# Spreading k's rows with a 0/1 matmul in an attention and feed-forward kernel

## The chip, the cores and the metric

The kernel runs on one core of a Trainium2 chip. The metric is device time in microseconds. The notes on each instruction come from one profiled execution of the kernel before.

## The reference, cut to what matters

One transformer layer on `x` of 4096 tokens by 256, all in float32:

```
q, k, v = x@Wq.T+bq, x@Wk.T+bk, x@Wv.T+bv      # 16 heads of 16 columns each
q, k    = rope(q), rope(k)                     # (xr, xi) -> (xr*c - xi*s, xr*s + xi*c)
x = layernorm(x + (softmax(q @ k.T / 16) @ v) @ Wo.T)
x = layernorm(x + ffn(x))                      # 256 -> 1024 -> 1024 -> 1024 -> 256
```

## The kernel before

There are three stages, each a block of five engine programs with a barrier behind it: `project` (L78), `attend` (L327), `feed_forward`. Constants: CH = 512 tokens in a chunk, NCH = 8 chunks, P = 128, HD = 16, FT = 2 halves of the 256 features, PAIRS = 8 pairs of heads.

`project` makes four *items* in each chunk, m = 0 to 3: q and k of the first feature half, q and k of the second (t = m % 2 is 1 for k). An item is [128 features, 512 tokens].

- PE (L216): for each item two float32 matmuls into `ps[m]` (each is two MATMUL instructions in the trace), then v for the chunk (`ps_v`, L239, L242).
- ACT (L255): the item's bias, `ps` to `item` (L262), and the copies of v to `v_all` (L269). There is a ring of four `item` and `ps` buffers; the bias of item n waits until item n-4 is split (`low_done`).
- DVE (L295) and POOL (L212): the rotation. DVE swaps neighbours (L303) and multiplies by the cosines (L305), POOL multiplies the swapped copy by the sines, DVE adds (L309). The rotated item is then split into a rounded *high* part (L287) and the *rest* (L292). The split of item n-1 is written inside item n: its high part behind L305, its rest behind L309 of item n.
- SP (L142): loads x and the tables; stores both parts of every item, q's and k's, to DRAM (`store`, L153) and reads k's back (`place`, `place_k`, L67), six DMAs for each k item. A `parts` buffer is free again only when its store has landed, and there is one for q and one for k. At the end SP waits for all of it (L195, L197).

`place_k` lays the rows out as the scores need them. `k_all` has two halves of 64 partitions, one for each head of a pair: 48 rows of k (high, rest, high of its 16 features), then three rows of ones, then 13 that nothing reads. The last k item is placed at the start of `attend` (L422), and the ones are written there by two DMAs from a buffer that POOL fills (L464, L430).

`attend` works in 32 units of (chunk, group of four heads). PE makes all the scores once for the row maxima (`wide`, L507), which DVE reduces (L646); the negated maxima go through POOL into three rows of `q_sb` (L413); PE makes the scores again with those rows (L572), ACT takes the exponential (L624), PE sums with v (L532). At its start stand 64 groups of maxima of unit 0 and the first 8 of unit 1; only then comes `unit(0, 0)`. SP's order there: q (L75), the last of k (L67), more q, the ones (L430), a copy of the feed-forward weights (L432), then, for each unit, some words of those weights (L439) and the shift rows (L413). DVE's scan of the words (L666) stands between the maxima of units 0 and 1.

Of the kernel before, what the change touches and what calls it, by code (L numbers as in the profile page):

```python
# [16 lines left out]
F32 = mybir.dt.float32  # L17
# [39 lines left out]
PLACES = PAIR * len(K_PART)  # L57


def place_k(sp, k_parts, k_all, c, ft, done):  # L60
    cols = bass.ds(c * CH, CH)
    pairs = slice(ft * PAIRS // FT, (ft + 1) * PAIRS // FT)
    for e in range(PAIR):
        for r, part in enumerate(K_PART):
            src = k_parts[part].rearrange("(j e d) s -> e d j s", e=PAIR, d=HD)[e]
            at = e * HALF + r * HD
            sp.dma_start(k_all[at:at + HD, pairs, cols].bitcast(F32), src[:, pairs, cols]).then_inc(done, 16)  # L67
# [10 lines left out]
def project(nc, io, parts_dram, v_all, k_all):  # L78

    with ExitStack() as ctx:
# [9 lines left out]
        RING = 4  # L96
# [9 lines left out]
        parts = [sb(f"parts{b}", [P, 2, CH], F32R) for b in range(2)]  # L106
# [16 lines left out]
        parts_free = [sem(f"parts_free{b}") for b in range(2)]  # L123
        k_in = sem("k_in")
        v_ready = sem("v_ready")
        v_free = sem("v_free")
        waited = sem("project_waited")
        sp_waited = sem("sp_waited")
        ones_set = sem("ones_set")

        ITEMS = 2 * FT
        TOTAL = NCH * ITEMS

        def started(n):

            return not isinstance(n, int) or 0 <= n < TOTAL
# [4 lines left out]
        def _(sp):  # L141
            def load(p, c):  # L142
                cols = bass.ds(c * CH, CH)
# [4 lines left out]
            def store(c, m):  # L148

                ft, t = m // 2, m % 2  # L150
                sp.wait_ge(low_done, RING + c * ITEMS + m + 1)
                dst = parts_dram[t].rearrange("a f s -> f a s")[ft * P:(ft + 1) * P]
                sp.dma_start(dst[:, :, bass.ds(c * CH, CH)], parts[t][:].bitcast(F32)).then_inc(parts_free[t], 16)  # L153

            def place(c, ft):

                sp.wait_ge(parts_free[1], 16 + (c * FT + ft + 1) * 16)
                sp.sem_inc(sp_waited, 1)
                place_k(sp, parts_dram[1], k_all, c, ft, k_in)

            def chunk(c, first=False):
                store(c, 0)
                if not first:
                    place(c - 1, 1)
                store(c, 1)
                store(c, 2)
                place(c, 0)
                store(c, 3)

            sp.dma_start(w_sb[:, 0], io["wqT"].rearrange("(t p) o -> p t o", p=P)).then_inc(w_in, 16)  # L170
            load(0, 0)
# [7 lines left out]
            load(1, 1)  # L179
            chunk(0, first=True)  # L180
            sp.wait_ge(v_ready, 2)
            load(0, 2)
            chunk(1)
            sp.wait_ge(v_ready, 4)
            load(1, 3)
            with sp.Fori(1, NCH // 2 - 1) as cc:
                for p in range(2):
                    chunk(cc * 2 + p)


                    sp.wait_ge(v_ready, (cc * 2 + p + 1) * 2)
                    load(p, cc * 2 + p + 2)
            chunk(NCH - 2)
            chunk(NCH - 1)
            for b in range(2):  # L195
                sp.wait_ge(parts_free[b], 16 + 16 * TOTAL // 2)
            sp.wait_ge(k_in, 16 * PLACES * (NCH * FT - 1))  # L197

        @block.gpsimd
        def _(pool):  # L200
            pool.memset(v_all[:, :, :, :, HD:HD + 1], 1.0).then_inc(ones_set, 1)
            pool.wait_ge(ones_set, 1)
            pool.memset(one_row[:], 1.0).then_inc(ones_set, 1)
            pool.wait_ge(ones_set, 2)
            with pool.Fori(0, NCH // 2) as cc:
                for p in range(2):
                    pool.wait_ge(table_in[p], cc * 32 + 32)
                    for m in range(ITEMS):
                        n = (cc * 2 + p) * ITEMS + m

                        pool.wait_ge(swapped, n + 1)
                        pool.tensor_tensor(pair[m % 2][:], pair[m % 2][:], table[p][:, 1], ALU.mult).then_inc(sine_done, 1)  # L212

        @block.tensor
        def _(pe):
            def chunk(c, p):  # L216
                for m in range(ITEMS):
                    ft, t = m // 2, m % 2
                    n = c * ITEMS + m
                    if isinstance(c, int) and c == 0 and m < 2:  # L220

                        pe.wait_ge(w_in, 16 * (t + 1))
                    if started(n - RING):

                        pe.wait_ge(biased, n - RING + 1)
                    for i in range(FT):
                        last = pe.matmul(ps[m][:], w_sb[:, t, i, ft * P:(ft + 1) * P], xt[p][:, i],  # L227
                                         start=(i == 0), stop=(i == FT - 1))
                    last.then_inc(projected, 1)
                if isinstance(c, int) and c == 0:  # L230
                    pe.wait_ge(v_weights_in, 32)
                    pe.wait_ge(ones_set, 2)
                for a in range(2):

                    pe.wait_ge(v_free, c * 2 + a + 1)
                    for b in range(2):
                        tt = 2 * a + b
                        for i in range(FT):
                            pe.matmul(psv[a][:, b], xt[p][:, i, tt * P:(tt + 1) * P], wv_sb[:, i],  # L239
# [5 lines left out]
            for p in range(2):  # L245
                pe.wait_ge(x_in[p], 16)
                chunk(p, p)
            with pe.Fori(1, NCH // 2) as cc:
                for p in range(2):
                    pe.wait_ge(x_in[p], cc * 16 + 16)  # L250
                    chunk(cc * 2 + p, p)

        @block.scalar
        def _(act):
            def chunk(c):  # L255
                for m in range(ITEMS):
                    ft, t = m // 2, m % 2
                    n = c * ITEMS + m
                    act.wait_ge(projected, n + 1)

                    act.wait_ge(low_done, n + 1)
                    act.activation(item[m][:], ps[m][:], ACT.Identity, bias=b_sb[:, t, ft:ft + 1]).then_inc(biased, 1)  # L262
                    if m >= ITEMS - 2:

                        a = m - (ITEMS - 2)
                        act.wait_ge(v_ready, c * 2 + a + 1)
                        for b in range(2):
                            dst = v_all[:, :, bass.ds(c * TT + 2 * a + b, 1), :, 0:HD]
                            last = act.activation(dst.rearrange("p g a j d -> p (g a) j d"),  # L269
                                                  psv[a][:, b].rearrange("p (g j d) -> p g j d", g=NG, j=HG), ACT.Copy)  # L270
                        last.then_inc(v_free, 1)

            act.wait_ge(b_in, 32)
            chunk(0)
            chunk(1)
            with act.Fori(2, NCH) as c:
                chunk(c)
            act.wait_ge(v_free, 2 + 2 * NCH)

        @block.vector  # L280
        def _(dve):
            def high(n, b):

                if started(n):
                    dve.wait_ge(rotated, n + 1)
                    dve.wait_ge(parts_free[b % 2], (n - b % 2) * 8 + 16)
                    dve.tensor_copy(parts[b % 2][:, 0], item[b][:]).then_inc(high_done, 1)  # L287

            def low(n, b):
                if started(n):  # L290
                    dve.wait_ge(high_done, n + 1)
                    dve.tensor_tensor(parts[b % 2][:, 1], item[b][:], parts[b % 2][:, 0].bitcast(F32), ALU.subtract)\  # L292
                        .then_inc(low_done, 1)

            def chunk(c, p):  # L295
                for m in range(ITEMS):
                    n = c * ITEMS + m
                    if started(n - 2):
# [3 lines left out]
                    dve.sem_inc(waited, 1)  # L302
# [3 lines left out]
                    high(n - 1, (m - 1) % RING)  # L306
# [3 lines left out]
                    low(n - 1, (m - 1) % RING)  # L310

            dve.sem_inc(low_done, RING)
            dve.sem_inc(v_free, 2)
            for b in range(2):
                dve.sem_inc(parts_free[b], 16)
            for p in range(2):
                dve.wait_ge(table_in[p], 32)
                chunk(p, p)
            with dve.Fori(1, NCH // 2) as cc:
                for p in range(2):  # L320
                    dve.wait_ge(table_in[p], cc * 32 + 32)
                    chunk(cc * 2 + p, p)
# [924 lines left out]
```

## Time and profile before

| what | us |
|---|---|
| median of 3 runs | 3895.44 (3888.07 to 3899.75) |
| the profiled execution | 3898.05 |
| its span, first to last instruction | 3896.5 |
| PE, DVE, ACT busy in the span | 3556.2, 2932.8, 2469.0 |
| granted PE clock, mean | 0.939 of full |

Busy shares are means over stages with different limits. The stages in the trace: `project` to 173 us, `attend` from 173.5 us, `feed_forward` at the end.

### The profile page before, as it was taken

The numbers are of one execution on the slowest core, as the hardware profiler recorded it, in microseconds if no ns is written. First come the engines' busy times: TensorE is split into PE (matmuls) and PEld (weight loads), VectorE is DVE, ScalarE is ACT, GpSimd is POOL, SyncE is SP. The second block draws the span as 40 slices with busy tenths as digits, with TensorE's granted clock in tenths as the row PEclk, the third lists the DMA queues.
The fourth block names the chain that finished last, engine by engine and source line by source line (L and its number), as shares of the span: only waits on it lengthen the run. The fifth ranks groups of instructions, "written<-read, shape, count | busy, mean of one in ns | idle before, by whom it ended". The sixth has DMA issues, their size and how long they took to land. (4 is left out here: it accounts for less than half of the span.)

```text
span 3896.5 us, 63480 instructions
## 1 busy us (share of the span) xinstructions
PE 3556.2 (91%) x20130; PEld 1524.5 (39%) x20130; DVE 2932.8 (75%) x3148; ACT 2469.0 (63%) x4472; POOL 197.3 (5%) x352
## 2 busy tenths in 40 slices
PE   7679999999999999999999999999988869999999
PEld 3222333332333323332332333222222148888887
DVE  6688888888888888888888888888886035445554
ACT  2118888877778878887877887778787522222222
POOL 3200000000000000000000000000000011111100
PEclk9759999999999999999999999999999579999999
DMA  8940000000000000000000000000000051000100
GB/s 212 201 133 12 12 12 12 12 12 12 23 12 12 12 12 12 12 12 13 22 12 12 12 12 12 12 12 12 12 14 4 0 181 34 34 33 33 49 17 12
DMA packets 64516, 125.61 MB, mean 32 GB/s; under 512 B 12551, under 2 KB 24904, under 8 KB 63032
## 3 DMA queue, kind: packets, MB, share of 16 engines
q1 hardware_dynamic: 59528, 114.02, 10.4%
q0 software_dynamic: 4704, 7.81, 0.7%
q8 instruction: 177, 2.90, 0.3%
q14 instruction: 107, 0.88, 0.1%
HBM read 90.59 MB, written 41.16 MB: 34 GB/s over the span
## 5 line engine op out<-in xcount | busy, mean ns | idle before, releaser
L646 DVE TENSOR_REDUCE group_max<-wide 128x2 f32<-128x1024 f32 x2048 | 2405.8, 1220 | 365.2 <-PE wide L507 364.3
L624 ACT ACTIVATE probs<-scores 128x512 f32<-128x512 f32 x4096 | 2227.1, 596 | 583.8 <-PE scores L572 491.6
L572 PE MATMUL scores<-q_sb,k_all 51*128 51x512 f32 x4096 | 1064.7, 516 | 197.5 <-ACT probs L624 60.3
L532 PE MATMUL sums<-probs,v_all 128*17 128x512 f32 x8192 | 1135.0, 627 | 0.0
L572 PEld LDWEIGHTS scores<-q_sb,k_all 51*128 51x128 f32 x4096 | 395.8, 190 | 1460.2 <-ACT probs L624 1362.7
L507 PE MATMUL wide<-k_all,q_sb 48*128 48x512 f32 x4096 | 809.2, 461 | 75.5 <-DVE group_max L646 49.2
L507 PEld LDWEIGHTS wide<-k_all,q_sb 48*128 48x128 f32 x4096 | 404.3, 194 | 381.9 <-DVE group_max L646 347.7
L1029 ACT ACTIVATE whole_hid<-acc,scale 128x512 f32<-128x512 f32 x128 | 84.9, 690 | 346.5 <-PE acc L910 344.9
L910 PE MATMUL acc<-hid_b,h2T 128*128 128x512 f32 x1024 | 241.6, 396 | 0.0
L910 PE MATMUL acc<-hid_a,h1T 128*128 128x512 f32 x1024 | 240.2, 394 | 0.0
L532 PEld LDWEIGHTS sums<-probs,v_all 128*17 128x17 f32 x8192 | 137.1, 96 | 262.5 <-ACT probs L624 197.3
L910 PEld LDWEIGHTS acc<-hid_b,h2T 128*128 128x128 f32 x1024 | 192.2, 188 | 46.5
L910 PEld LDWEIGHTS acc<-hid_a,h1T 128*128 128x128 f32 x1024 | 191.7, 187 | 47.2
L1119 DVE CAST hid_a<-whole_hid 128x512 fp32r<-128x512 f32 x128 | 54.5, 426 | 185.5 <-ACT whole_hid L1029 183.4
L474 POOL CAST shift_parts<-shift 16x128 bf16<-16x128 f32 x32 | 9.1, 285 | 2741.6 <-ACT shift L617 2662.9
L1020 ACT ACTIVATE gate<-acc,scale 128x512 f32<-128x512 f32 x64 | 44.3, 691 | 125.2 <-PE acc L910 120.8
L1180 DVE TENSOR_SCALAR flag<-flip 1x1 int32<-1x1 f32 x1 | 0.1, 145 | 147.2 <-PE flip L997 147.2
L227 PE MATMUL ps_qk<-xt,w_qk 128*128 128x512 f32 x128 | 73.4, 738 | 26.7 <-DMA xt<-in_xT 26.7
L1121 DVE TENSOR_TENSOR hid_a<-whole_hid,hid_a 128x512 fp32r<-128x512 f32 x128 | 88.7, 693 | 4.4
L1128 DVE SCALAR_TENSOR_TENSOR whole_hid<-acc,scale,gate 128x512 f32<-128x512 f32 x64 | 48.0, 750 | 45.3 <-PE acc L910 45.2
L883 PE MATMUL tok<-wo,heads_sb 128*128 128x256 f32 x256 | 58.7, 389 | 18.0 <-DVE heads_sb L1094 18.0
L910 PE MATMUL acc<-x1t,w1T 128*128 128x512 f32 x256 | 71.8, 402 | 2.1 <-DVE x1t L1113 2.1
(77 smaller groups left out, 1158.4 us busy)
## 6 DMA issues: line engine op xcount, KB each, us to landing
k_all<-k_parts SPq DMA_DIRECT2D x96, 128.0 KB, 5.0
q_sb<-q_parts SPq DMA_DIRECT2D x192, 64.0 KB, 2.3
w_words<-ff_weights SPq DMA_DIRECT2D x32, 352.0 KB, 3.2
q_parts<-parts SPq DMA_DIRECT2D x16, 512.0 KB, 5.7
k_parts<-parts SPq DMA_DIRECT2D x16, 512.0 KB, 6.2
heads<-mixed SPq DMA_DIRECT2D x32, 256.0 KB, 2.5
heads_sb<-heads SPq DMA_DIRECT2D x8, 1024.0 KB, 4.9
shares<-shares_dram POOLq DMA_DIRECT2D x112, 64.0 KB, 2.2
```

Of the source, the lines that this page charges most:

```text
L227: last = pe.matmul(ps[m][:], w_sb[:, t, i, ft * P:(ft + 1) * P], xt[p][:, i], start=(i == 0), stop=(i == FT - 1))
L507: last = pe.matmul(wide[n % 2][:, e], q_sb[g][rows, j, t * P:(t + 1) * P], k_all[rows, g * GP + j, b * CH:(b + 1) * CH], start=True, stop= ...
L532: last = pe.matmul(sums[32 * j:32 * j + HD + 1, :], v_all[:, g, kt, j], probs[(kt * HG + j) % RING][:], start=(kt == 0), stop=(kt == KT - 1))
L572: pe.matmul(scores[(s + e) % BANKS][:], k_all[rows, g * GP + j, kt * P:(kt + 1) * P], q_sb[g][rows, j], start=True, stop=True).then_inc(sc ...
L624: act.activation(probs[n % RING][:], scores[s % BANKS][:], ACT.Exp, scale=INV_SCALE)\
L646: dve.reduce_max(group_max[:, n], wide[n % 2][:], AX_X).then_inc(wide_free, 1)
L883: last = pe.matmul(tok[t // 2][:, t % 2], heads[:, g, t * P:(t + 1) * P], wo[:, g], start=(g == 0), stop=(g == NG - 1))
L910: mm = pe.matmul(dst, w.bitcast(view), src[h].bitcast(view), start=(first and h == 0), stop=(last and h == 1))
L1029: act.activation(whole[o % 4][:], acc[n % 4][:], ACT.Gelu, scale=scale[:, 2 + layer, o:o + 1])\
L1119: dve.tensor_copy(dst[0][:, k % HT], whole[k % 4][:]).then_inc(rounded, 1)
L1121: dve.tensor_tensor(dst[1][:, k % HT], whole[k % 4][:], dst[0][:, k % HT].bitcast(F32), ALU.subtract)\
L1128: dve.scalar_tensor_tensor(out=whole[o % 4][:], in0=acc[(2 * o + 1) % 4][:], scalar=scale[:, 1, o:o + 1], in1=gate[o % 2][:], op0=ALU.mult ...
```

## The change

k's parts stay on the chip. `choose` is a 0/1 matrix, [128, 2, 128]: for each pair of heads j, its 32 rows by 128 columns send the high and rest rows of two heads to their places in a [128, 512] PSUM tile. ACT copies that tile to `k_all` with a bias of one in the rows of ones. The matrix is made at the start by POOL and DVE. q still goes through DRAM. All loops over chunks in `project` are written out. The items' order against the new `spread_k` is the same on PE and ACT. Cut to its core (`load`, the item's own operations and what only lost its register arithmetic are left out):

```diff
-def place_k(sp, k_parts, k_all, c, ft, done):
...
-        RING = 4
+        RING, SPREADS = 4, 2
+        spread = [psum(f"ps_spread{b}", [P, CH]) for b in range(SPREADS)]
...
+            for c in range(NCH):                         # sync
+                for ft in range(FT):
+                    sp.wait_ge(low_done, c * ITEMS + 2 * ft + 1)
+                    dst = q_dram.rearrange("a f s -> f a s")[ft * P:(ft + 1) * P]
+                    sp.dma_start(dst[:, :, c * CH:(c + 1) * CH], parts[0][:].bitcast(F32)).then_inc(q_stored, 16)
+                if c + 2 < NCH:
+                    sp.wait_ge(v_ready, 2 * c + 2)
+                    sp.wait_ge(rotated, (c + 1) * ITEMS)
+                    load(c + 2)
+            sp.wait_ge(q_stored, 16 * NCH * FT)
...
+            def spread_k(c, ft):                         # tensor; JP = 4
+                if c == 0 and ft == 0:
+                    pe.wait_ge(choose_set, 5)
+                pe.wait_ge(low_done, c * ITEMS + 2 * ft + 2)
+                for j in range(JP):
+                    i = (c * FT + ft) * JP + j
+                    rows = slice(j * PAIR * HD, (j + 1) * PAIR * HD)
+                    if i >= SPREADS:
+                        pe.wait_ge(spread_free, i - SPREADS + 1)
+                    for a in range(2):
+                        last = pe.matmul(spread[i % SPREADS][:], choose[rows, a], parts[1][rows, a],
+                                         start=(a == 0), stop=(a == 1))
+                    last.then_inc(spread_ready, 1)
+            for c in range(NCH):
+                pe.wait_ge(x_in[c % 2], (c // 2 + 1) * 16)
+                item_of(c, 0)
+                item_of(c, 1)
+                if c > 0:
+                    spread_k(c - 1, 1)
+                item_of(c, 2)
+                item_of(c, 3)
+                values(c)
+                spread_k(c, 0)
+            spread_k(NCH - 1, 1)
...
+            def spread_k(c, ft):                         # scalar
+                for j in range(JP):
+                    i = (c * FT + ft) * JP + j
+                    act.wait_ge(spread_ready, i + 1)
+                    act.activation(k_all[:, ft * JP + j, c * CH:(c + 1) * CH], spread[i % SPREADS][:], ACT.Identity,
+                                   bias=ones_rows[:]).then_inc(spread_free, 1)
...
+            def high(n):                                 # vector
+                t, b = n % 2, n % RING
+                dve.wait_ge(rotated, n + 1)
+                if t == 0 and n >= 2:
+                    dve.wait_ge(q_stored, 16 * (n // 2))
+                if t == 1 and n >= 2:
+                    dve.wait_ge(spread_ready, JP * (n // 2))
+                dve.tensor_copy(parts[t][:, 0], item[b][:]).then_inc(high_done, 1)
...
-            place_k(sp, k_parts, k_all, NCH - 1, FT - 1, k_in)      # attend
-            sp.wait_ge(ones_set, 1)
-            (two DMAs of ones into k_all, and the waits on k_in and k_ones)
```

ACT's loop over chunks has the same order as PE's: bias 0, bias 1, `spread_k(c - 1, 1)`, bias 2, bias 3, the copies of v, `spread_k(c, 0)`.

## Rows read from the trace of the kernel before

**Rows 1.** Busy time by stretch, within project (us, engines, clock, DMA).

```profile
39.01:44.76 5.75, 5.75 (x7) 2.52 (x8) 5.12 (x11) 0.69 (x1) 1.93 (x2) 0.50 1.08 250
58.33:61.80 3.47, 3.47 (x4) 1.45 (x5) 1.66 (x4) 0.00 (x0) 1.77 (x1) 0.51 1.07 300
77.64:97.86 20.22, 15.97 (x41) 7.83 (x41) 13.22 (x25) 3.97 (x8) 7.08 (x4) 0.84 1.01 235
```

**Rows 2.** Waits in 20 to 175 us: who, for whom, us, times, longest.

```profile
DVE parts L287 <- DMA k_parts<-parts: 35.0, 14, 3.5
PE ps_qk L227 <- DMA xt<-in_xT: 20.9, 6, 4.2
```

**Rows 3.** Timeline of PE, projections by chunk: start, length, [idle before it].

```profile
21.77 7.13 PE L227 MATMUL ps_qk<-xt,w_qk 128*128 128x512 f32 x16
39.01 9.97 PE L227 MATMUL ps_qk<-xt,w_qk 128*128 128x512 f32 x16 [3.56 <-DMA xt<-in_xT]
58.33 8.82 PE L227 MATMUL ps_qk<-xt,w_qk 128*128 128x512 f32 x16 [2.81 <-DMA xt<-in_xT]
137.04 8.74 PE L227 MATMUL ps_qk<-xt,w_qk 128*128 128x512 f32 x16 [3.25 <-DMA xt<-in_xT]
```

**Rows 4.** Timeline, all engines, of the first chunks.

```profile
23.07 0.72 DVE L303 STREAM_SHUFFLE pair<-item 128x512 f32<-128x512 f32 x1
...
23.79 0.69 ACT L262 ACTIVATE item<-ps_qk,b_qk 128x512 f32<-128x512 f32 x1 [1.25 <-PE ps_qk L227]
...
25.51 0.69 ACT L262 ACTIVATE item<-ps_qk,b_qk 128x512 f32<-128x512 f32 x1 [1.03 <-PE ps_qk L227]
...
26.44 0.68 DVE L292 TENSOR_TENSOR parts<-item,parts 128x512 fp32r<-128x512 f32 x1
...
27.05 0.71 DVE L303 STREAM_SHUFFLE pair<-item 128x512 f32<-128x512 f32 x1
...
28.74 1.03 PE L239 MATMUL ps_v<-w_v,xt 128*128 128x256 f32 x4
...
34.75 0.69 PE L242 MATMUL ps_v<-b_v,one_row 1*128 1x256 f32 x2
...
35.48 0.66 ACT L269 ACTIVATE v_all<-ps_v 128x256 f32<-128x256 f32 x2 [2.13 <-PE ps_v L242]
```

**Rows 5.** Timeline of PE in attend: fp32r matmuls at half clock, then at full.

```profile
182.79 0.80 PE L507 MATMUL wide<-k_all,q_sb 48*128 48x512 f32 x2 [0.34 <-DVE group_max L646]
...
278.70 1.05 PE L532 MATMUL sums<-probs,v_all 128*17 128x512 f32 x8
279.69 0.50 PE L572 MATMUL scores<-q_sb,k_all 51*128 51x512 f32 x2
280.02 0.70 PE L507 MATMUL wide<-k_all,q_sb 48*128 48x512 f32 x4
```

**Rows 6.** Waits of SP's own queue, 0 to 280 us.

```profile
SPq L197 <- DMA k_parts<-parts: 5.9, 1, 5.9
```

**Rows 7.** Timeline, all engines, first load and first matmul of attend.

```profile
173.52 2.65 SPq L75 DMA_DIRECT2D q_sb<-q_parts  x6
...
178.43 1.22 PE L507 MATMUL wide<-k_all,q_sb 48*128 48x512 f32 x4 [26.09 <-DMA q_sb<-q_parts]
```

**Rows 8.** Timeline, all engines, from the ones to attend's first unit.

```profile
187.92 1.76 SPq L430 DMA_DIRECT2D k_all<-mixed  x2
...
254.02 0.37 SPq L439 DMA_DIRECT2D w_words<-ff_weights  x1
255.87 4.22 SPq L413 DMA_DIRECT2D q_sb<-shift_rows  x6
257.04 0.89 DVE L666 SCALAR_TENSOR_TENSOR bits<-w_words,bits 128x704 int32<-128x704 int32 x1 [4.40 <-DMA w_words<-ff_weights]
257.85 11.40 DVE L646 TENSOR_REDUCE group_max<-wide 128x2 f32<-128x1024 f32 x10
...
264.94 0.34 PEld L572 LDWEIGHTS scores<-q_sb,k_all 51*128 51x128 f32 x2
```

More of the change, by code:

```diff
@@ L56 @@
 SLOT = SHIFT_ROW + 3
-PLACES = PAIR * len(K_PART)
-def place_k(sp, k_parts, k_all, c, ft, done):
[L61 to L67, printed above, removed]
+PLACES = PAIR * len(Q_PART)
 def place_q(sp, q_parts, q_sb, c, g, done):
@@ L75, in place_q, with project @@
             sp.dma_start(q_sb[at:at + HD].bitcast(F32), src[:, g * GP:(g + 1) * GP, bass.ds(c * CH, CH)]).then_inc(done, 16)
-def project(nc, io, parts_dram, v_all, k_all):
+def project(nc, io, q_dram, v_all, k_all):
     with ExitStack() as ctx:
@@ L105, in project @@
         pair = [sb(f"pair{b}", [P, CH]) for b in range(2)]
-        parts = [sb(f"parts{b}", [P, 2, CH], F32R) for b in range(2)]
+        parts = [sb(f"parts{t}", [P, 2, CH], F32R) for t in range(2)]
+        eye = sb("eye", [P, P])
+        same = sb("same", [P, PAIR * HD])
+        choose = sb("choose", [P, 2, P], F32R)
+        ones_rows = sb("ones_rows", [P, 1])
         ps = [psum(f"ps_qk{b}", [P, CH]) for b in range(RING)]
         psv = [psum(f"ps_v{a}", [P, 2, D]) for a in range(2)]
+        spread = [psum(f"ps_spread{b}", [P, CH]) for b in range(SPREADS)]
         w_in = sem("w_qk_in")
@@ L122, in project @@
         low_done = sem("low_done")
-        parts_free = [sem(f"parts_free{b}") for b in range(2)]
-        k_in = sem("k_in")
+        q_stored = sem("q_stored")
+        spread_ready = sem("spread_ready")
+        spread_free = sem("spread_free")
         v_ready = sem("v_ready")
         v_free = sem("v_free")
-        waited = sem("project_waited")
-        sp_waited = sem("sp_waited")
         ones_set = sem("ones_set")
+        eye_set = sem("eye_set")
+        choose_set = sem("choose_set")
         ITEMS = 2 * FT
         TOTAL = NCH * ITEMS
-        def started(n):
-            return not isinstance(n, int) or 0 <= n < TOTAL
+        JP = PAIRS // FT
         block = ctx.enter_context(nc.Block())
@@ L141, in _, with load @@
         def _(sp):
-            def load(p, c):
-                cols = bass.ds(c * CH, CH)
+            def load(c):
+                cols, p = slice(c * CH, (c + 1) * CH), c % 2
                 sp.dma_start(xt[p][:], io["xT"].rearrange("(t p) s -> p t s", p=P)[:, :, cols]).then_inc(x_in[p], 16)
@@ L146, in load @@
                     sp.dma_start(table[p][:, n], io[name][:, cols]).then_inc(table_in[p], 16)
[L148 to L168, printed above, removed]
             sp.dma_start(w_sb[:, 0], io["wqT"].rearrange("(t p) o -> p t o", p=P)).then_inc(w_in, 16)
-            load(0, 0)
+            load(0)
             for n, name in enumerate(["bq", "bk"]):
@@ L178, in _ @@
             sp.dma_start(bv_sb[:], io["bv"].rearrange("(o d) -> o d", o=1)).then_inc(v_weights_in, 16)
[L179 to L197, printed above, removed]
+            load(1)
+            for c in range(NCH):
[8 more added lines that the diff above has]
+            sp.wait_ge(q_stored, 16 * NCH * FT)
         @block.gpsimd
@@ L203, in _ @@
             pool.memset(one_row[:], 1.0).then_inc(ones_set, 1)
[L204 to L212, printed above, removed]
+            pool.memset(eye[:], 0.0).then_inc(eye_set, 1)
@@ new lines, in _ @@
+            pool.memset(choose[:].bitcast(F32), 0.0).then_inc(choose_set, 1)
+            pool.wait_ge(eye_set, 1)
+            pool.affine_select(out=eye[:], in_=eye[:], compare_op=ALU.not_equal, fill=1.0, base=0,
+                               pattern=[[-1, P]], channel_multiplier=1).then_inc(eye_set, 1)
+            for c in range(NCH):
+                p = c % 2
+                pool.wait_ge(table_in[p], (c // 2 + 1) * 32)
+                for m in range(ITEMS):
+                    pool.wait_ge(swapped, c * ITEMS + m + 1)
+                    pool.tensor_tensor(pair[m % 2][:], pair[m % 2][:], table[p][:, 1], ALU.mult).then_inc(sine_done, 1)
@@ L214, in _, with item_of @@
         @block.tensor
         def _(pe):
[L216 to L230, printed above, removed]
+            def item_of(c, m):
+                ft, t, n = m // 2, m % 2, c * ITEMS + m
+                if c == 0 and m < 2:
+                    pe.wait_ge(w_in, 16 * (t + 1))
+                if n >= RING:
+                    pe.wait_ge(biased, n - RING + 1)
+                for i in range(FT):
+                    last = pe.matmul(ps[m][:], w_sb[:, t, i, ft * P:(ft + 1) * P], xt[c % 2][:, i],
+                                     start=(i == 0), stop=(i == FT - 1))
+                last.then_inc(projected, 1)
@@ L231, in chunk, with values @@
+            def values(c):
+                if c == 0:
                     pe.wait_ge(v_weights_in, 32)
@@ L238, in chunk @@
                         for i in range(FT):
-                            pe.matmul(psv[a][:, b], xt[p][:, i, tt * P:(tt + 1) * P], wv_sb[:, i],
+                            pe.matmul(psv[a][:, b], xt[c % 2][:, i, tt * P:(tt + 1) * P], wv_sb[:, i],
                                       start=(i == 0), stop=False)
@@ L243, in chunk @@
                     last.then_inc(v_ready, 1)
[L245 to L251, printed above, removed]
+            def spread_k(c, ft):
[11 more added lines that the diff above has]
+                    last.then_inc(spread_ready, 1)
@@ L253, in _ @@
+            for c in range(NCH):
+                pe.wait_ge(x_in[c % 2], (c // 2 + 1) * 16)
+                item_of(c, 0)
+                item_of(c, 1)
+                if c > 0:
+                    spread_k(c - 1, 1)
[4 more added lines that the diff above has]
+            spread_k(NCH - 1, 1)
         @block.scalar
         def _(act):
[L255 to L271, printed above, removed]
@@ L273, in _, with bias @@
-            act.wait_ge(b_in, 32)
[L274 to L278, printed above, removed]
+            def bias(c, m):
+                ft, t, n = m // 2, m % 2, c * ITEMS + m
+                act.wait_ge(projected, n + 1)
+                if n >= RING:
+                    act.wait_ge(low_done, n - RING + 1)
+                act.activation(item[m][:], ps[m][:], ACT.Identity, bias=b_sb[:, t, ft:ft + 1]).then_inc(biased, 1)
@@ new lines, in values @@
+            def values(c):
+                for a in range(2):
+                    act.wait_ge(v_ready, c * 2 + a + 1)
+                    for b in range(2):
+                        dst = v_all[:, :, c * TT + 2 * a + b, :, 0:HD]
+                        last = act.activation(dst, psv[a][:, b].rearrange("p (g j d) -> p g j d", g=NG, j=HG), ACT.Copy)
+                    last.then_inc(v_free, 1)
+            def spread_k(c, ft):
[4 more added lines that the diff above has]
+                                   bias=ones_rows[:]).then_inc(spread_free, 1)
@@ L280, in _ @@
+            act.wait_ge(b_in, 32)
+            act.wait_ge(choose_set, 6)
+            for c in range(NCH):
+                bias(c, 0)
+                bias(c, 1)
+                if c > 0:
+                    spread_k(c - 1, 1)
+                bias(c, 2)
+                bias(c, 3)
+                values(c)
+                spread_k(c, 0)
+            spread_k(NCH - 1, 1)
+            act.wait_ge(v_free, 2 * NCH)
+            act.wait_ge(spread_free, NCH * FT * JP)
         @block.vector
         def _(dve):
[L282 to L295, printed above, removed]
+            def high(n):
[6 more added lines that the diff above has]
+                dve.tensor_copy(parts[t][:, 0], item[b][:]).then_inc(high_done, 1)
@@ new lines, in low @@
+            def low(n):
+                t, b = n % 2, n % RING
+                dve.wait_ge(high_done, n + 1)
+                dve.tensor_tensor(parts[t][:, 1], item[b][:], parts[t][:, 0].bitcast(F32), ALU.subtract)\
+                    .then_inc(low_done, 1)
+            dve.wait_ge(eye_set, 2)
+            dve.wait_ge(choose_set, 1)
+            dve.reduce_max(same[:], eye[:].rearrange("p (j x) -> p x j", x=PAIR * HD), AX_X).then_inc(choose_set, 1)
+            dve.wait_ge(choose_set, 2)
+            for r, part in enumerate(K_PART):
+                dst = choose[:, part].rearrange("p (e r d) -> p e r d", e=PAIR, d=HD)[:, :, r]
+                dve.tensor_copy(dst, same[:].rearrange("p (e d) -> p e d", e=PAIR)).then_inc(choose_set, 1)
@@ L296, in chunk @@
+            by_half = eye[:].rearrange("p (e x) -> p e x", e=PAIR)[:, :, SHIFT_ROW:SLOT]
+            dve.reduce_max(ones_rows[:], by_half, mybir.AxisListType.XY).then_inc(choose_set, 1)
+            for c in range(NCH):
+                p = c % 2
+                dve.wait_ge(table_in[p], (c // 2 + 1) * 32)
                 for m in range(ITEMS):
                     n = c * ITEMS + m
-                    if started(n - 2):
+                    if n >= 2:
                         dve.wait_ge(rotated, n - 1)
@@ L309, in chunk, with attend @@
                     dve.tensor_tensor(item[m][:], item[m][:], pair[m % 2][:], ALU.add).then_inc(rotated, 1)
[L310 to L322, printed above, removed]
-            high(TOTAL - 1, (TOTAL - 1) % RING)
-            low(TOTAL - 1, (TOTAL - 1) % RING)
-def attend(nc, io, q_parts, k_parts, heads_dram, w_dram, low_bits, v_all, k_all):
+                    if n >= 1:
+                        low(n - 1)
+            high(TOTAL - 1)
+            low(TOTAL - 1)
+def attend(nc, io, q_parts, heads_dram, w_dram, low_bits, v_all, k_all):
     with ExitStack() as ctx:
@@ L421, in _ @@
             load_q(0, 0)
-            place_k(sp, k_parts, k_all, NCH - 1, FT - 1, k_in)
             for g in range(1, NG):
                 load_q(0, g)
-            sp.wait_ge(ones_set, 1)
-            for e in range(PAIR):
-                at = e * HALF + SHIFT_ROW
-                rows = k_all[at:at + 3].rearrange("a j (c s) -> a (j c) s", s=CH)
-                src = mixed[0][0:3].unsqueeze(1).to_broadcast([3, PAIRS * NCH, CH])
-                sp.dma_start(rows.bitcast(F32), src).then_inc(k_ones, 16)
             for name, (at, rows, cols) in W_AT.items():
@@ L517, in max_start @@
             def max_start(c, g):
-                if not isinstance(c, int) or g >= NG // FT:
-                    pe.wait_ge(k_in, 16 * PLACES)
                 pe.wait_ge(q_in[g], c * (16 * PLACES) + 16 * PLACES)
@@ L1197, in build @@
 def build(nc, io, out):
-    parts_dram = [nc.dram_tensor(f"{t}_parts", [2, D, S], F32, kind="Internal").ap() for t in "qk"]
+    q_dram = nc.dram_tensor("q_parts", [2, D, S], F32, kind="Internal").ap()
     heads_dram = nc.dram_tensor("heads", [NCH, P, NG, CH], F32, kind="Internal").ap()
@@ L1206, in build @@
             with nc.sbuf_tensor("k_all", [P, PAIRS, S], F32R) as k_all:
-                project(nc, io, parts_dram, v_all, k_all)
-                attend(nc, io, *parts_dram, heads_dram, w_dram, low_bits, v_all, k_all)
+                project(nc, io, q_dram, v_all, k_all)
+                attend(nc, io, q_dram, heads_dram, w_dram, low_bits, v_all, k_all)
         feed_forward(nc, io, heads_dram, shares_dram, w_dram, low_bits, out)
```

11 lines of the change are left out of this document (3 added, 8 removed).

## The prediction

> **What bounds the kernel now.** I read the table of stretches first, then the waits, then the timeline of a chunk, then the two ends of the stage.
>
> `attend` and `feed_forward` hold 3723 of the 3896.5 us. The change touches them at `attend`'s start alone: the loops keep their instructions but for a wait that has long been met. So the question is how long `project` lasts and how `attend` starts.
>
> In `project` the chunks begin 19.6 us apart: (137.04 - 39.01)/5 [rows 3]. DMA sets that. Its engines are busy for all of a chunk (share 1.01) at 235 GB/s [rows 1], DVE waits 35.0 us for k's stores to land, and PE 20.9 us for x [rows 2]. PE alone would need less: at full clock one item takes 25.51 - 23.79 = 1.72 us, and the v part runs from 28.74 to 34.75 + 0.69 = 35.44, 6.7 us [rows 4], so a chunk 4 x 1.72 + 6.7 = 13.6 us. DVE and POOL need 27.05 - 23.07 = 3.98 us an item [rows 4], 15.9 us a chunk. After each wait for x PE's granted clock is at the lower level (0.50, 1.2 GHz) for 3.5 to 5.8 us of dense work [rows 1]; idle stretches of 2.81 and of 3.56 us both went before it [rows 3].
>
> **What goes.** In each chunk two stores of k (512 KB each) and twelve reads back (128 KB each), 2.5 MB of 4.5 MB. What stays, 2 MB (1 MB of x and tables, two q stores), is 9 us at 235 GB/s, hidden in any chunk of 20 us. DVE's wait for k's landings goes. If nothing else bound the chunk, DVE would, at 15.9 us. What is late next is, I think, not an engine but a ring of orders.
>
> **What comes, and the ring.** The rest of item (c-1, 3) is made inside DVE's item (c, 0), behind its add. `spread_k(c-1, 1)` waits for it on PE, which works in order, so the items (c, 2) and (c, 3), v, `spread_k(c, 0)` and item (c+1, 0) are all queued behind that wait. DVE's item (c+1, 0), in which the next such rest is made, waits for the last of these. One turn of the ring is one chunk. I time it from the start of DVE's item (c, 0), S = 0, at full clock.
>
> - The rest is ready 26.44 + 0.68 - 23.07 = 4.05 us after the item's start [rows 4]; with some 0.1 to pass the semaphore, PE starts at 4.15.
> - A spread is two fp32r matmuls of 512 columns, one after the other in one bank. Two pairs take 0.70, one pair 0.50 [rows 5], so a stream of 512 columns costs some 0.215, and a spread 0.43; ACT starts 0.3 later (an item's end on PE against its bias: 21.77 + 1.72 against 23.79 [rows 3, 4]). The nearest row for the copy is the bias, PSUM to SBUF with a per-row operand, 0.69 [rows 4]; I let two in a row start 0.61 apart. With two buffers the third spread waits for the first copy. Copies start at 4.88, 5.49, 6.38 and 6.99; PE's four spreads end at 6.69, and not at 4.15 + 4 x 0.43 = 5.87.
> - Item 2 ends at 8.41, its bias runs 8.71 to 9.40, so DVE's item 2 starts at 9.54 (it could have at 7.96). Item 3 ends at 10.13, v at 16.83. `spread_k(c, 0)` needs the rest of item 1, ready at 13.6: no wait. Its first copy stands behind two copies of v (0.66 [rows 4]) and starts at 17.74; two buffers again, and PE ends its fourth spread at 19.54.
> - Item (c+1, 0) ends at 21.26, its bias runs 21.56 to 22.25, DVE starts at 22.39.
>
> That is 22.4 us for a chunk at full clock, against 19.6 now. If the spreads waited for no copy, 2 x 0.95 would go: 20.5, still over 19.6. Dearer spreads are bounded by a half-clock one, 0.85.
>
> Clock: item (c+1, 1) ends on PE at 22.98 and the next rest is ready at 26.54. PE is idle 3.6 us in every chunk, between the idle stretches that now go before the lower level [rows 3]. I take the same here: lower level for a mean of 4.7 us of work behind the gap (between the 3.5 and the 5.8 of [rows 1]). At half clock a pair takes 0.80 [rows 5]; a spread is 0.85, is ready 0.35 later, and the four end 3.67 after their start instead of 2.54: 1.13 lost. The 1.0 us left of the lower level falls on item 2: 0.5 lost. Together 1.65 (bounds: 0 where the clock stays, 2.9 where the lower level lasts 6.8 us).
>
> Between full-array matmuls and others PE loses a little: eight sums and the start of the next scores lie 0.99 apart where the sums stream for 4 x 0.215 = 0.86 [rows 5], 0.13 lost. A spread phase has two such borders, one of the four hidden behind the wait: 3 x 0.1 = 0.3 (bounds 0 and 0.4).
>
> The Trainium skill has a rule for this that speaks against the change: TensorEngine Tiling, "Key Properties", says that going from one tiling mode to another drains TensorE. The 0.13 us agrees with a small price; by that row all four borders would cost 0.5 us a chunk.
>
> So a chunk takes 22.4 + 1.65 + 0.3 = 24.35 us.
>
> **Start and end of the stage.** Chunk 0 goes as now up to DVE's item 2 at 23.07 - 3.98 = 19.1 [rows 4]: `choose` needs some ten small operations of POOL and DVE, which have nothing else to do before the first bias. The rest of item 1 comes at 23.1; spreads to 25.8, item (1, 0) to 27.5, DVE's item (1, 0) at 28.6 (now 27.05 [rows 4]). Item (7, 0) starts at 28.6 + 6 x 24.35 = 174.7. The last chunk ends with eight copies: PE's v at S + 18.5, copies from 19.4, the first four with starts 0.6 to 0.9 apart, the other four by 25.2. The last q store is issued at S + 19.2 and lands by 24 (SP now waits 5.9 us for k's last [rows 6]). Then some 0.9 for the barrier, an estimate: a few waits of the 0.1 us kind in a row, bounds 0.3 and 2. SP's first q load: 174.7 + 25.2 + 0.9 = 200.8, against 173.52 [rows 7]: 27.3 later.
>
> **`attend`'s start.** Six DMAs of k (2.7 us of SP's queue, as the six of q) and two of ones (1.76) go [rows 7, 8]. q's load to the first matmul, 4.9 us [rows 7], and the 64 groups of maxima stay, as DVE bounds them (1.14 us each by the ten at 257.85 [rows 8]). The copy of the weights is issued 4.5 us sooner after the first q load, and DVE's scan now waits 4.40 us for its words, whose load waited for that copy to 254.02 [rows 8]. So DVE resumes up to 4.2 us sooner. PE's first scores stand behind the 8 groups of unit 1 that DVE paces to 264.94; the shift rows, issued from 255.87 with 4.22 us of issue [rows 8], land near 262. I take 264.94 - 262.2 = 2.7 us gained (bounds 0 and 4.2). k's waits in the loops and the instructions of the written-out loops I take as nothing: PE's queue hides the former, and chunks 0 and 1, written out already, show no stall.
>
> **Sum.** +27.3 - 2.7 = +24.6. The profiled execution's 3898.05 becomes 3922.7; the median shown lies 2.6 lower, so 3920.
>
> **The rivals.**
>
> 1. *The clock stays at its upper level.* For it: the gap is shared between two stretches of work, and spreads begin at once. Against: 2.81 us were enough [rows 3]. Chunk 22.7, last chunk 23.5: item (7, 0) at 164.8, q load at 189.2, +15.7 - 2.7 = +13; 3908.
> 2. *The lower level covers more than I take*, since a spread uses 32 of 128 rows and waits for ACT between. Then `spread_k(c, 0)` and item (c+1, 0) run at half clock too: 1.13 + 1.72 = 2.85 more, less what overlaps: 26.5 to 27.2. Item (7, 0) at 28.6 + 6 x 26.9 = 190, +42.6 - 2.7 = +40; 3936. The fp32r matmuls at 182.79 stay at half clock though PE is idle 0.34 of each 1.13 us [rows 5], which speaks for it; the items between, dense for 10 us, against.
> 3. *The ring does not close*: the new time is that of the freed engines. The place is PE's wait ahead of item (c, 2); if the rest of (c-1, 3) came before PE gets there, a chunk would be PE's sum, 13.6 + 16 x 0.215 = 17.0, and the kernel faster. Item (7, 0) at 131, last chunk 23: q load at 155, -19 - 2.7 = -21; 3874. It decides below 19.6 us a chunk. The DMA share speaks for it [rows 1]; the order of DVE's program, in which that rest stands behind the add of an item that PE has yet to feed, against it.
> 4. *The change is lost in the noise*: copies cheaper than 0.69 and half-free spreads, a chunk near 20.5. Item (7, 0) at 151.6, q load at 176, +2 - 3 = 0; 3895.
>
> **How the numbers follow.** A difference under 0.3%, 11.7 us, can't be told from no change. The forecast 0.52, rival 1 0.17 (of which some 0.07 within 0.3%), rival 2 0.13, rival 3 0.08, rival 4 0.10. So slower 0.74, same 0.18, faster 0.08. The range takes in rivals 1 and 2 and the three runs' own spread of 12 us: 3903 to 3938.
>
> **What would show it.** In the new trace: DVE's items 0 of two chunks 24 us apart; its items 2 and 0 each waiting on ACT's bias, some 1.6 to 3.2 and 5 us; PE idle 3.6 us ahead of `spread_k(c-1, 1)` with DVE's L292 as releaser; half clock once a chunk; DMA share near 0.5; the first q load near 200; the scan's wait under 1 us. PE idle ahead of item 2 under 1 us, or chunks under 20 us apart, would prove the ring wrong; a stage of 24 us a chunk and a total within 12 us of now would prove the part on `attend` wrong.

## The result, and the profile after

The changed kernel takes 3963.73 us (3953.64 to 3969.86, 4 runs) against 3893.85 (4 runs) for the kernel before: 1.0178 [1.0155, 1.0202], slower by 70 us. I had forecast 3920, 25 us slower, in a range up to 3938. The sign was right, the size was not, and the time lies outside the range.

The page of the kernel after (span, busy, granted clock):

```profile
span 3964.0 us, 63316 instructions
PE 3623.9 (91%) x20258; PEld 1551.2 (39%) x20258; DVE 2953.4 (75%) x3153; ACT 2506.5 (63%) x4536; POOL 196.5 (5%) x354
PEclk8858999999999999999999999999998579999999
DMA  2240000000000000000000000000000051111100
```

The same row of the kernel before:

```profile
DMA  8940000000000000000000000000000051000100
```

DMA's share in the first two slices is 2 tenths, where it was 8 and 9: the transfers did go off the path. PE's mean clock is a little lower than before: 0.80 from 20 us to the end of `project`, against 0.83.

One chunk of `project` in the kernel after, from DVE's item (4, 0) to item (5, 0), then its pieces by clock. The columns are those of [rows 1]: the stretch, its length, the busy us of PE, PEld (weight loads), DVE, ACT and POOL with the number of instructions, PE's clock, DMA's share and GB/s:

```profile
113.04:140.34 27.30, 22.39 (x57) 10.53 (x57) 15.98 (x25) 9.12 (x16) 7.02 (x4) 0.81 0.23 77
112.00:118.80 6.80, 2.75 (x10) 1.01 (x9) 5.70 (x10) 2.26 (x4) 2.67 (x2) 1.00 0.00 1
118.80:125.60 6.80, 6.80 (x10) 2.94 (x11) 2.88 (x5) 2.43 (x4) 0.81 (x1) 0.50 0.20 77
125.60:135.90 10.30, 9.44 (x36) 5.25 (x35) 7.39 (x11) 3.76 (x9) 3.54 (x2) 1.00 0.20 55
135.90:139.30 3.40, 3.40 (x5) 1.33 (x6) 0.00 (x0) 0.67 (x2) 0.00 (x0) 0.51 0.86 296
```

A chunk takes 27.3 us, not 19.6 and not the 24.35 forecast. PE works at half clock in two stretches, 6.8 and 3.4 us; before there was one, of 3.4 or 6.8 us. DMA's share of a chunk is 0.23.

PE's timeline of that chunk, with its idle time before each group:

```profile
117.15 0.73 PE L220 MATMUL ps_spread<-parts,choose 32*128 32x512 f32 x4 [3.28 <-DVE parts L294]
118.65 1.80 PE L220 MATMUL ps_spread<-parts,choose 32*128 32x512 f32 x4 [0.77 <-ACT k_all L260]
120.38 6.28 PE L187 MATMUL ps_qk<-xt,w_qk 128*128 128x512 f32 x8
126.50 1.03 PE L202 MATMUL ps_v<-w_v,xt 128*128 128x256 f32 x4
...
134.53 1.31 PE L220 MATMUL ps_spread<-parts,choose 32*128 32x512 f32 x4 [0.86 <-ACT k_all L260]
135.77 5.40 PE L187 MATMUL ps_qk<-xt,w_qk 128*128 128x512 f32 x8
```

The ring is there: PE stands 3.28 us until DVE's rest (L294), 4.11 us after the start of DVE's item. The two items behind the spreads take 126.50 - 120.38 = 6.1 us, where they take 3.44 at full clock.

The waits of the kernel after in 20 to 240 us, against [rows 2]:

```profile
DVE pair L315 <- ACT item L245: 74.4, 14, 7.3
PE ps_spread L220 <- DVE parts L294: 26.3, 9, 3.3
PE ps_spread L220 <- ACT k_all L260: 13.0, 16, 0.9
```

DVE's waits for stores are gone; it waits 74.4 us for biases (items written by ACT) instead, in 14 places, some two a chunk.

The start of `attend` after, against [rows 7, 8] (timeline, SP and DVE):

```profile
224.07 13.03 SPq L65 DMA_DIRECT2D q_sb<-q_parts  x24
...
274.18 0.37 SPq L431 DMA_DIRECT2D w_words<-ff_weights  x1
...
303.20 0.87 DVE L652 SCALAR_TENSOR_TENSOR bits<-w_words,bits 128x704 int32<-128x704 int32 x1
306.51 4.21 SPq L412 DMA_DIRECT2D q_sb<-shift_rows  x6
...
311.89 0.80 PE L559 MATMUL scores<-q_sb,k_all 51*128 51x512 f32 x2 [0.18 <-DMA q_sb<-shift_rows]
```

The two spans differ by 3964.0 - 3896.5 = 67.5 us, and this is where they are. The first q load comes 224.07 - 173.52 = 50.5 later. From it to unit 0's shift rows both kernels take 82.4. From there to unit 1's it is 89.8 against 95.3: 5.5 gained. The next 30 units take 2658.5 against 2641.9: 16.6 lost. The end of `attend` takes 2.5 and the feed-forward (from its first load of x, at 3199.99 and 3135.79) 3.3 more. The 16.6 were in no step of mine:

```profile
PE wide L498 <- issue: 13.0, 6, 2.4
```

That is a row of the kernel after's waits in 330 to 2950 us: six times PE stands up to 2.4 us with nothing that it waits for. The kernel before has two such stalls there (`PE scores L572 <- issue: 7.2, 2, 3.7`). One of the six in the timeline of PE:

```profile
755.50 0.39 PE L498 MATMUL wide<-k_all,q_sb 48*128 48x512 f32 x1
758.28 1.22 PE L498 MATMUL wide<-k_all,q_sb 48*128 48x512 f32 x3 [2.39 <-issue]
758.98 0.94 PE L559 MATMUL scores<-q_sb,k_all 51*128 51x512 f32 x2
759.85 1.91 PE L519 MATMUL sums<-probs,v_all 128*17 128x512 f32 x8
```

It lies in the second group of matmuls of the loop's first unit, one loop turn (four units) from the next. Behind it eight sums take 1.91 us, not the 1.05 of [rows 5]: the clock has fallen.

### The profile page after: what moved, and what is told of

Its sections match the earlier page's. It is cut to its first block and busy times, and to the rows that moved or that the text cites. A ratio compares the mean times of both kernels' runs of the same rounds, so it can differ in the third digit from the quotient of the medians.

```text
span 3964.0 us, 63316 instructions
## 1 busy us (share of the span) xinstructions
PE 3623.9 (91%) x20258; PEld 1551.2 (39%) x20258; DVE 2953.4 (75%) x3153; ACT 2506.5 (63%) x4536; POOL 196.5 (5%) x354
## 5 line engine op out<-in xcount | busy, mean ns | idle before, releaser
L498 PE MATMUL wide<-k_all,q_sb 48*128 48x512 f32 x4096 | 817.9, 463 | 63.8 <-DVE group_max L632 44.3
L187 PE MATMUL ps_qk<-xt,w_qk 128*128 128x512 f32 x128 | 90.1, 868 | 6.0 <-DMA xt<-in_xT 6.0
L220 PE MATMUL ps_spread<-parts,choose 32*128 32x512 f32 x128 | 40.9, 534 | 39.2 <-DVE parts L294 26.3
```

What stands on the lines that cost most here:

```text
L498: last = pe.matmul(wide[n % 2][:, e], q_sb[g][rows, j, t * P:(t + 1) * P], k_all[rows, g * GP + j, b * CH:(b + 1) * CH], start=True, stop= ...
```

## The experiments

All were timed beside the kernel before on the same chip.

| kernel | us, median | ratio to before [95%] | a chunk | first q load | units 2 to 31 |
|---|---|---|---|---|---|
| after_again | 3966.68 | 1.0169 [1.0153, 1.0186] | 27.3 | 222.8 | 2660.4 |
| fill_gap | 3947.17 | 1.0128 [1.0112, 1.0145] | 27.3 | 219.2 | 2638.7 |
| fill_spread | 3933.82 | 1.0098 [1.0079, 1.0118] | 25.6 | 213.5 | 2632.4 |
| fill_all | 3913.70 | 1.0034 [1.0023, 1.0046] | 22.5 | 192.4 | 2644.2 |
| order | 3936.53 | 1.0099 [1.0082, 1.0116] | 21, 21, 26 | 195.0 | 2653.8 |
| early | 3929.23 | 1.0080 [1.0063, 1.0097] | 21 to 24 | 189.6 | 2651.7 |
| pad32 | 3943.13 | 1.0114 [1.0098, 1.0131] | 27.3 | 224.8 | 2636.9 |
| pad96 | 3959.87 | 1.0156 [1.0139, 1.0173] | 27.3 | 233.9 | 2647.4 |
| before_pad32 | 3902.18 | 1.0013 [1.0003, 1.0023] | 18.9 to 20.6 | 174.3 | 2642.7 |
| inter | 3879.20 | 0.9948 [0.9931, 0.9964] | 17.2 to 18.7 | 160.0 | 2636.4 |

"A chunk" is the distance of DVE's items 0 in the profile, in the later chunks; "units 2 to 31" goes from the first shift DMA of unit 1 to that of unit 31.

### after_again

> The changed kernel once more, for a second profile. All theories: some 70 us over the kernel before. Theory A (the projection costs 50 us, and the rest, +13 us in attend and +3 in the feed-forward, is the chance of where the clock's drops fall): the chunks of project lie 27.3 us apart again, the 30 later units of attend sum to anything from 2635 to 2665 us. Theory B (attend itself is slower by the change): they sum to 2658 again, within 5 us.

The chunks repeat at 27.3 us, with half clock twice a chunk, but not with the same drops: here each of the two lasts 6.8 us, 13.7 in all against 10.2, and the first begins at 115.9, just ahead of the spreads.

```profile
111.89:139.17 27.28, 23.19 (x57) 11.14 (x57) 15.97 (x24) 9.12 (x16) 7.01 (x4) 0.75 0.23 77
```

The units sum to 2660.4, inside what both theories allow, so the sum alone decides nothing. The six stalls are back, though (12.6 us): they belong to this program, not to one execution.

### fill_gap, fill_spread, fill_all

```diff
+            def fill(n, cols, times):                 # w_k stands here for k's weights, read as [128, 512]
+                pe.wait_ge(biased, n + 1)
+                for _ in range(times):
+                    pe.matmul(ps[n % RING][:, 0:cols], w_sb[:, 0, 0, 0:P], w_k[:, 0:cols], start=True, stop=True)
...
             def spread_k(c, ft):
+                if ft == 1 and c < NCH - 1:               # fill_gap, fill_all
+                    fill(c * ITEMS + 2, CH, 3)
                 pe.wait_ge(low_done, c * ITEMS + 2 * ft + 2)
...
                     last.then_inc(spread_ready, 1)
+                    if j == 1 and c < NCH - 1:            # fill_spread, fill_all
+                        fill(c * ITEMS + 2 * ft, CH // 2, 2)
```

> The changed kernel with three more float32 matmuls of 512 columns (2.6 us at full clock) on PE ahead of its wait for the rest of the last k item, into a ps bank that has been read; their results are overwritten. PE is idle 3.3 us there now, so they cost nothing in themselves. Theory A (the ring costs 22.7 us a chunk at full clock, and the lower clock behind the idle stretch and behind the spreads the other 4.6): the 6.8 us of half clock behind the gap go or shrink to 3.4, a chunk takes 24 to 25.5, the kernel 15 to 25 us less than the changed one. Theory C (spreads, their latency and their semaphores are dearer than I took, the clock is not it): a chunk stays at 27.3.

> As fill_gap, and in each spread phase two more float32 matmuls of 256 columns (0.43 us at full clock) between the second and the third spread, where PE waits 0.8 us for ACT. Theory A: no half clock in project after the first chunk, a chunk 22.5 to 23.5, the kernel 30 to 38 us less than the changed one. Theory C: 27.3 or more.

> The changed kernel with the two small filler matmuls between the second and the third spread alone, none in the 3.3 us gap. Theory G (it is the idle gap that takes the clock down, the spread phases only keep it down): the drop behind the gap stays, 24 to 26 us a chunk, the other one (behind the spreads that follow v) goes. Theory H (it is the spread phases, since in fill_gap, whose gap is filled, both drops stayed in the later chunks): close to fill_all's 22.5. Either way no stall of PE in attend is expected, since the program is longer: total 3915 to 3935.

A chunk by stretch in fill_gap (PE's wait for DVE's rest is down to 0.71 us):

```profile
135.49:162.79 27.30, 24.98 (x63) 11.68 (x62) 16.00 (x25) 9.13 (x16) 7.02 (x4) 0.81 0.23 78
```

And in fill_all:

```profile
98.64:121.15 22.51, 21.79 (x71) 11.20 (x71) 16.00 (x25) 9.02 (x16) 7.02 (x4) 1.00 0.28 92
```

fill_all decides: with PE kept busy in both places the granted clock is 1.00, and the chunk is the ring at full clock, 22.52 us. PE has more work, and the first q load comes 30 us sooner (222.8 to 192.4). The other 4.8 us of the changed kernel's chunk are the clock. The same 32-row spreads are in fill_all, so their few rows alone don't take the clock down. The total fell by 53 us against after_again, more than the 30 to 38 I expected: of the rest 16 us lie in units 2 to 31, where this longer program has one stall of 3.0 us and not six.

Filling the gap alone leaves the chunk at 27.3 (theory C's number, though not for its reason), and the clock still falls in the middle of the spreads. Filling the spreads alone gives 25.6 with one drop of 6.8 us a chunk, as theory G had it. So neither G nor H holds for both: spreads with waits of 0.8 us between them are enough for a drop (fill_gap), and so is the gap (fill_spread). fill_gap's total fell within my 15 to 25 us, but for another reason: 3.6 us by the first q load (two early chunks were short), and one stall in `attend` instead of six.

### order, early

order moves `spread_k(c - 1, 1)` behind item 3, on PE and on ACT:

```diff
                 item_of(c, 0)
                 item_of(c, 1)
-                if c > 0:
-                    spread_k(c - 1, 1)
                 item_of(c, 2)
                 item_of(c, 3)
+                if c > 0:
+                    spread_k(c - 1, 1)
```

early splits each chunk's last item at once, on DVE:

```diff
-                    if n >= 1:
+                    if n >= 1 and m > 0:
                         high(n - 1)
...
-                    if n >= 1:
+                    if n >= 1 and m > 0:
                         low(n - 1)
+                high(n)
+                low(n)
```

> The changed kernel with the spread of the previous chunk's last k item moved behind the four items on PE and behind the four biases on ACT. Theory A (the ring through DVE's rest, with PE in order, is what sets the chunk): the ring opens, PE's 3.3 us of idle go, a chunk is PE's own sum, 18.6 us at full clock and up to 20.5 with one drop; project ends 50 to 68 us sooner than in the changed kernel, the total is 3895 to 3915. Theory C: PE's work is the same, so a chunk gains at most the 3.3 us of idle, 24 us.

> The changed kernel with the split of each chunk's last k item right behind its add on DVE, not inside the next chunk's first item. Theory A (the ring): PE no longer waits for it, the ring is open as in order, a chunk is PE's sum of 18.6 us and what the lower clock adds, 21 to 24; total 3925 to 3940, the six stalls in attend included. Theory C (the order of PE's work): no gain, 27.3.

Either opens the ring, by two different edits: 28 and 33 us less by the first q load than after_again. PE's wait for DVE's rest between 40 and 190 us, in the changed kernel and then in order (in early it is the same row):

```profile
PE ps_spread L220 <- DVE parts L294: 16.4, 5, 3.3
PE ps_spread L220 <- DVE parts L294: 1.3, 1, 1.3
```

But they stop at 21 us a chunk and more, and order's total missed my 3895 to 3915; early's came inside its 3925 to 3940. In order one chunk in three takes 26.0, at a mean clock of 0.67:

```profile
99.21:125.20 25.99, 24.44 (x56) 11.97 (x55) 15.90 (x24) 9.10 (x16) 7.02 (x4) 0.67 0.28 97
```

PE is busy 24.44 of 25.99 us there and still at the lower level for the most part. Both keep the six stalls in `attend` (13.7 us each): their PE programs have as many instructions as the changed one.

### pad32, pad96, before_pad32

```diff
+            for _ in range(32):                          # 96 in pad96
+                pe.sem_inc(pad, 1)
             for c in range(NCH):
                 pe.wait_ge(x_in[c % 2], (c // 2 + 1) * 16)
```

> The changed kernel with 32 semaphore increments more in PE's program, at its start, where PE waits for x anyway. Theory F (some 17 us of the loss are in attend, because PE's program is now laid out so that six times, at the loop's turn, PE stands 1.6 to 2.4 us without an instruction, and the clock falls behind it; where the loop lies against the pieces in which instructions are fetched decides): a shift of the layout changes the number or length of these stalls, by as much as all: the 30 later units sum to 2640 where they are gone, the kernel 3945 to 3950; project stays at 27.3 us a chunk. Theory B (it is k_all written by ACT, or the chance of the clock): the stalls stay, 3963 to 3967.

> As pad32 with 96 increments, about as many instructions as fill_gap had more. Theory F: fill_gap had no such stall, so here too they go: 3945 to 3950. Theory B: 3963 to 3967.

> The kernel before with 32 semaphore increments more at the start of PE's program, where PE waits for x. Theory F (layout of PE's program against the pieces in which it is fetched): the stalls at the loop's turn in attend change, the total by anything from -5 to +22 us with project the same. If the kernel before happens to lie as well as it can, it is unchanged within 0.3% or slower. Theory B: unchanged.

32 instructions that do nothing take 0.55% off the kernel (1.0114 against 1.0169), 21 us, with `project` unchanged. PE's row in the waits of pad32, 330 to 2950 us, where the changed kernel has six stalls:

```profile
PE scores L562 <- issue: 2.8, 1, 2.8
```

pad96 loses the stalls too (one, 2.9 us) but costs what I had not counted: 96 increments don't fit in PE's wait for x, and the first q load is 10 us later. 3959.9 less those 10 is 3950. The kernel before doesn't gain by the same shift: 1.0013, though its two stalls (7.2 us) are gone; PE's clock is at the lower level for 164 of the us from 330 to 2950, where it was 147. So a stall has no fixed price. Of the twelve profiles, units 2 to 31 take 2651.7 to 2660.4 us in the four with six stalls, and 2632.4 to 2647.4 in the eight with two, one or none.

What PE most likely waits for in a stall stands in the profile's records of DMA queue q8, which the page calls "instruction" (the kernel after, then before):

```profile
q8 instruction: 198, 3.24, 0.3%
q8 instruction: 177, 2.90, 0.3%
```

In each of the changed kernel's six stalls one 16 KB transfer of this queue ends, and PE goes on 1.3 to 1.4 us later (756.91 to 758.28 in the stall shown); the six stalls of after_again and the six of order end in the same way, 1.2 to 1.6 us behind such a transfer. At each of these turns three of them start within 10 us (14 at the most), where they mostly come some 20 us apart.

### inter

Each spread stands alone among other work:

```diff
+                        if c > 0:                        # in values(c), ahead of quarter tt of v
+                            one_k(c - 1, 1, tt)
...
             for c in range(NCH):                         # tensor
...
-                item_of(c, 0)
-                item_of(c, 1)
-                if c > 0:
-                    spread_k(c - 1, 1)
-                item_of(c, 2)
-                item_of(c, 3)
+                for m in range(ITEMS):
+                    item_of(c, m)
+                    if c > 0 and m < 2:
+                        one_k(c - 1, 0, 2 + m)
                 values(c)
-                spread_k(c, 0)
-            spread_k(NCH - 1, 1)
+                for j in range(2 if c < NCH - 1 else JP):
+                    one_k(c, 0, j)
+            for j in range(JP):
+                one_k(NCH - 1, 1, j)
```

`one_k(c, ft, j)` is one of the four spreads of `spread_k(c, ft)`. ACT's copies follow the same order.

> The changed kernel with one spread at a time between PE's other work: four of the previous chunk between the quarters of v, two behind v, two behind items 0 and 1, and ACT's copies in that order. PE's wait for ACT's copies (0.8 us in each spread phase) and for DVE's rest go. Theory A: a chunk is PE's streams, 17.1 us at full clock, DVE's 15.9 behind it; if the clock stays up project ends near 155 and the kernel takes 3875 to 3885; if the mix of small matmuls keeps it down for a part, 20 to 24 us a chunk and 3900 to 3935. Theory C: over 3935.

```profile
66.06:83.23 17.17, 17.06 (x58) 7.93 (x57) 14.13 (x25) 9.22 (x17) 7.05 (x4) 1.00 0.37 124
```

PE is busy 17.06 of 17.17 us at full clock: its streams, 17.1, set the chunk. (One later chunk takes 18.7, at a mean clock of 0.91.) The change done in this order is faster than the kernel before, 0.9948 [0.9931, 0.9964], 18 us.

## Why the prediction was wrong, step by step

- **What goes: right.** Stores, reads back and DVE's waits for them are gone. DMA's share is 0.23 of a chunk, less than the 0.5 forecast: the 2 MB that stay keep DMA busy for 6.3 us, not 9.
- **The ring: right, in place and size.** I worked out 22.4 us at full clock and 0.3 for the borders between full-array matmuls and others; fill_all has 22.52, which leaves 0.1 for the borders. PE starts the spread 4.11 us after DVE's item (4.15 forecast) and idles 3.28 us (3.6). DVE waits for the biases of items 2 and 0, as said. order and early open it.
- **The clock: the step that failed.** "I take the same here: lower level for a mean of 4.7 us of work behind the gap", 1.65 us a chunk. It is 10.2 us of lower level in two stretches (13.7 in after_again), and it costs 27.3 - 22.5 = 4.8 us a chunk. (My bound of 2.9 for 6.8 us of lower level is 2.7 by its own terms; either is too low.) I had carried over the gap's cost from a kernel with dense float32 work on either side. Here the level is up through the gap, falls in the middle of the spreads with their waits for ACT (in after_again at their start), and stays down until PE has done items 2 and 3; behind v and its spreads it falls a second time. By fill_gap the waits in the spreads are enough for both drops, and by fill_spread the gap is enough for one. This was rival 2, with 26.9 us and a chance of 0.13; against it I had argued with "the items between, dense for 10 us". They are dense, but the clock comes back only at the end of them, at 125.6, and falls again behind v.
- **Start and end of the stage: off, at the end by the same cause.** Item (1, 0) starts at 31.4, not 28.6; from item (7, 0) to the first q load it is 29.1, not 26.1. Together with six chunks 2.9 longer (17.4) that is the 23.2 us between 27.3 forecast and 50.5. In fill_all the end takes 26.3. Its item (1, 0) comes at 30.8 all the same, with PE's mean clock at 0.76 in the stretch before, as it is 0.73 in the changed kernel; that the clock makes the 2.8 us at the start is likely, and no run shows it.
- **`attend`'s start: right in kind.** SP's weights copy is done sooner (the words are asked for at 274.18, 50.1 us after the first q load, against 80.5; I had counted on 4.5 us), the scan waits no more, the first scores come 87.8 us after the load, against 91.4: 3.6 gained, 2.7 forecast.
- **"The instructions of the written-out loops I take as nothing": failed.** `attend`'s loop has the same matmuls, but PE's program ahead of it has another length, and PE stalls at the loop's turn: 13.0 us of stalls and the clock behind them, 17 us in the profile and 21 by pad32. Of the 21.6 us by which pad32's units 2 to 31 are shorter, 10.2 are stalls, and the lower level lasts 20 us less. The stalls end behind transfers of the instruction queue; why the number of instructions ahead of the loop decides whether they come stays open.

The sum mended, in the two spans: +27.3 forecast and +23.2 more for `project`, by the clock for the most part, -5.4 from the first q load to unit 1, +16.6 in the units behind it, +5.8 at the end of `attend` and in the feed-forward is 67.5. The few us in the feed-forward I leave to chance: it takes 760.7 to 764.6 us in the twelve profiles, with no order in it.

## What to carry to other kernels

Before calling a transfer the bound, write out the ring that is left when it goes: here one split, placed inside the next item, and an engine that works in order made 22.5 us out of engines that need 17.1. Give the clock a term of its own: here a phase of small matmuls that wait for their copies lowered the clock for the dense work behind it too, and the same matmuls put one by one among dense work did not. And when a long unrolling changes a stage, compare the stages that nobody touched, and shift the program by a few instructions before blaming their content.

## What the runs showed of the hardware

- More PE work made `project` 30 us shorter: 3.4 us of filler matmuls a chunk, at waits of 3.3 and 0.8 us, held the granted clock at 1.00 (fill_all). Fillers at only one of the places left it at the lower level for 6.8 us a chunk and more.
- A busy PE was not a PE at full clock: 24.44 of 25.99 us busy, mean clock 0.67 (order).
- The chunks of the changed kernel settle at the same length to 0.1 us, 27.3, in two profiles of it and in fill_gap, pad32 and pad96. The clock's drops lie at the same places in each chunk of a profile, but not in each profile: 10.2 us of lower level a chunk in four of them, 13.7 in after_again.
- 32 semaphore increments at the start of one engine's program changed stalls 700 us later, in a loop that they aren't part of, by 21 us in all. In each of the six stalls of the changed kernel PE went on 1.3 to 1.4 us after a 16 KB transfer of queue q8 had ended.
- ACT's copy of 128x512 from PSUM into a float32r tile took 0.69 us, as the bias did; a spread of two 32-row matmuls 0.43 us of stream at full clock.
